# Edge attention on one core: where the picking one-hots are made, how many columns are picked by products, and who empties the product bank

## The reference, cut to what matters

```python
h = jnp.maximum(_layernorm(x, axis=-1), 0.0)
# three times, with nf = h at first:
f_out = (nf @ W_ni)[src] + (nf @ W_nj)[dst] + ef @ W_fij + bias
f_out = leaky_relu(f_out, 0.2).reshape(-1, H, D)
e = einsum('ehd,hd->eh', f_out, attn)
a = exp(e - segment_max(e, dst)[dst]); a = a / segment_sum(a, dst)[dst]
hn = (nf @ W_node).reshape(-1, H, D)
nf = segment_sum(hn[src] * a[:, :, None], dst).mean(axis=1)
ef = f_out.mean(axis=1)
# at the end: x + nf
```

## Time and profile before

| | |
|---|---|
| median of 3 runs | 2908.23 us (2904.49 to 2915.27) |
| profiled execution, its own time | 2908.63 us |
| its span in the profile | 2906.8 us |
| TensorE busy | 2274.3 us, 78% |
| VectorE busy | 2435.2 us, 84% |
| ScalarE busy | 1503.3 us, 52% |
| GpSimd busy | 2060.1 us, 71% |
| mean granted clock of TensorE | 0.892 |

### The profile page before, as it was taken

How to read it: one execution, slowest core, us unless ns; L and a number is a source line. 1 busy time by engine, 2 the same in 40 slices (tenths; PEclk the granted TensorE clock), 3 DMA queues, 4 the chain that set the end, 5 groups by cost and what they waited for, 6 DMA issues and landing times.

```text
span 2906.8 us, 49919 instructions
## 1 busy us (share of the span) xinstructions
PE 2274.3 (78%) x15871; PEld 1753.4 (60%) x16027; DVE 2435.2 (84%) x5972; ACT 1503.3 (52%) x3713; POOL 2060.1 (71%) x2167
## 2 busy tenths in 40 slices
PE   3388888888888468888888887836888888888884
PEld 1266666666665356666666665535767666666653
DVE  7299999999997458999999998736898899898874
ACT  0056565656565225656565655613555555555552
POOL 6777777777772577777777777567777777777753
PEclk9699999999998689899999999958898898898885
DMA  7235454545442324444444443333334343343322
GB/s 256 69 97 160 116 158 119 161 116 159 118 132 93 106 68 143 118 139 140 138 134 140 142 138 103 106 112 96 103 103 124 115 128 106 114 127 102 103 89 80
DMA packets 139273, 353.90 MB, mean 122 GB/s; under 512 B 43895, under 2 KB 96027, under 8 KB 120207
## 3 DMA queue, kind: packets, MB, share of 16 engines
q1 hardware_dynamic: 67216, 296.09, 28.7%
q0 software_dynamic: 68960, 39.71, 9.3%
q10 hardware_dynamic: 2838, 14.91, 1.3%
HBM read 137.79 MB, written 212.77 MB: 121 GB/s over the span
## 4 chain that ended last, share of the span: by engine, by line
DVE 40%; PE 20%; issue 14%; ACT 12%; POOL 9%; DMA 3%; SPq 1%; DVEq 0%; ACTq 0%; POOLq 0%
DVE U L1383 17%; POOL rows L561 7%; DVE rows L1304 6%; PE f_ps L702 6%; DVE lr L1315 5%; PE f_ps L711 5%; DVE U L1368 4%; PE pick_ps L671 4%; ACT up L928 3%; ACT xT L848 3%; ACT f_low L857 3%; PE xT_ps L692 2%; DVE z L1394 2%; DVE rows L1405 2%; PE f_ps L721 2%
## 5 line engine op out<-in xcount | busy, mean ns | idle before, releaser
L561 POOL DMA_INDIRECT rows<-nf_tab,src_sb x1995 | 1890.8, 948 | 638.0 <-issue 588.0
L711 PEld LDWEIGHTS f_ps<-w_out,lr 128*128 128x128 f32 x4836 | 658.8, 201 | 357.7 <-issue 201.2
L1383 DVE TENSOR_TENSOR_SCAN U<-wide_ps,U 128x272 f32<-128x272 f32 (+2 forms) x1272 | 801.3, 692 | 3.3 <-ACT wide_ps L916 2.4
L702 PE MATMUL f_ps<-xT,w_edge 97*128 97x512 f32 x1212 | 697.7, 659 | 39.1 <-ACT ef_new L879 26.3
L671 PE MATMUL pick_ps<-nf_part,z 125*128 125x160 bf16 x6345 | 565.2, 247 | 208.4 <-issue 166.5
L671 PEld LDWEIGHTS pick_ps<-nf_part,z 125*128 125x128 bf16 x6345 | 507.8, 104 | 236.7 <-issue 189.7
L711 PE MATMUL f_ps<-w_out,lr 128*128 128x36 f32 (+1 forms) x4836 | 627.4, 269 | 27.2 <-DVE lr L1315 24.7
L1315 DVE TENSOR_TENSOR lr<-f_ps,f_low 128x512 f32<-128x512 f32 x606 | 407.5, 672 | 203.6 <-ACT f_low L857 202.9
L857 ACT ACTIVATE f_low<-f_ps 128x512 f32<-128x512 f32 x606 | 361.6, 597 | 325.6 <-PE f_ps L702 325.5
L692 PE MATMUL xT_ps<-ident,rows 128*97 128x128 f32 x2418 | 416.1, 297 | 92.1 <-issue 37.0
L916 ACT ACTIVATE wide_ps<-e_dw 128x289 f32<-128x289 f32 (+2 forms) x636 | 245.3, 402 | 348.7 <-DVE U L1383 343.0
(11 more groups left out here) (162 smaller groups left out, 1148.5 us busy)
## 6 DMA issues: line engine op xcount, KB each, us to landing
u_tab<-up SPq DMA_DIRECT2D x144, 1088.0 KB, 4.5
s_nd<-edge_first SPq DMA_DIRECT2D x48, 768.0 KB
rows<-nf_tab,src_sb POOLq DMA_INDIRECT x1995, 2.4
ef_tab<-ef_new SPq DMA_DIRECT2D x32, 768.0 KB
ef_st<-ef_tab SPq DMA_DIRECT2D x32, 768.0 KB
z<-fifth_tab SPq DMA_DIRECT2D x141, 96.0 KB
edge_first<-s_nd ACTq DMA_DIRECT2D x16, 768.0 KB
ef_st<-in_edge_attr_dram SPq DMA_DIRECT2D x16, 672.0 KB
```

Source lines behind the costliest of these rows:

```text
L561: eng.indirect_dma_start(rows[q % RING][:, c * K:c * K + D], None, nf_tab[:, :], bass.IndirectOffsetOnAxis(ap=src_sb[:, t:t + 1], axis=0)) ...
L702: eng.matmul(f_ps[n % 2][:, 0:grp_w(g) * P], w_edge[l][:, :], xT[y][0:K, 0:grp_w(g) * P], start=True, stop=True).then_inc(f_ready, 1)
L711: mm = eng.matmul(f_ps[n % 2][:, u * m:(u + 1) * m], lr[y][:, u * P:(u + 1) * P], w_out[l][:, 0:m], start=True, stop=True)
L1383: last = eng.tensor_tensor_scan(uh[:, c0 * w:c1 * w], dbc[h % 2][:, 0:(c1 - c0) * w], uh[:, c0 * w:c1 * w], 0.0, ALU.mult, ALU.add)
```

## The change

Every group from 6 to 182 has its column 2 picked (a batch is column 2 of three consecutive groups), and the first six groups have all four columns picked (eight batches, one for each column of three groups); a layer so has 67 batches and 605 gathers, not 47 and 665. Batches are picked nine ahead (START). The one-hots are made in the first layer alone: SP stores each to `hot_tab`, and in layers two and three loads it back (`load_hot`); three one-hot tiles take the place of two, two tiles of loaded columns the place of four. `take_picks` gains a second ScalarE copy, of the other four candidates to `pick_sb` in SBUF; `pick_rows` reads from there, and TensorE waits for both copies (`drained`) in place of VectorE's overwrites.

```diff
-LEAD = 8
-LEAD0 = 20
+LEAD = 14
+LEAD0 = 26
-HEADC = 48
-HEADM = 56
-HEAD_PACE = {16: 3, 24: 8, 32: 13, 40: 18}
+HEADC = 72
+HEADM = 80
+HEAD_PACE = {32: 3, 44: 8, 56: 13, 64: 18}
-IDXB = 4
+IDXB = 2
+HOTS = 3
+FRONT = 6
...
-    NPICK = END // GB + 1
+    WHOLE = FRONT // PICK * GT
+    AHEAD = 3
+    NPICK = WHOLE + (END - FRONT) // PICK
+    PEND = FRONT + (END - FRONT) // PICK * PICK
+    START = WHOLE - FRONT // PICK + AHEAD
...
+    hot_tab = nc.dram_tensor("hot_tab", (NPICK * NQ, PARTS5 * PICK * P), BF16, kind="Internal").ap()
...
+        pick_sb = sb("pick_sb", [P, PICK * (PB - D)])
+        rest4 = pick_sb[:, :].rearrange("p (c b d) -> p c b d", b=PARTS5 - 1, d=D)
...
         def is_picked(t):
-            return t % GT == 2 and picks(t // GT)
+            return t < FRONT * GT or (t % GT == 2 and t < PEND * GT)
...
+                def store_hot(b):
+                    eng.wait_ge(hot_made, PARTS5 * (b + 1))
+                    eng.dma_start(hot_tab[b * NQ:(b + 1) * NQ, :], hot[b % HOTS][0:NQ, :]
+                                  ).then_inc(hot_out[b % HOTS], 16)
+                def load_hot(l, b):
+                    m = l * NPICK + b
+                    eng.wait_ge(pick_ready, PICK * (m - HOTS + 1))
+                    if m < NPICK + HOTS:
+                        eng.wait_ge(hot_out[m % HOTS], 16 * -(-(NPICK - m % HOTS) // HOTS))
+                    eng.dma_start(hot[m % HOTS][0:NQ, :], hot_tab[b * NQ:(b + 1) * NQ, :]
+                                  ).then_inc(hot_in[m % HOTS], 16)
+                def bring(l, b):
+                    if l:
+                        load_hot(l, b)
+                        return
+                    m = b
                     if m >= IDXB:
-                        eng.wait_ge(hot_made, PARTS5 * (m - IDXB + 1))
+                        store_hot(m - IDXB)
                     eng.dma_start(fifths[m % IDXB],
...
-                    for b in range(IDXB + 2):
-                        load_fifths(l, b)
+                    loaded = START - 2 if l else IDXB + 2
+                    for b in range(loaded):
+                        bring(l, b)
                     load_first(q0)
                     load_first(q0 + 1)
+                    for b in range(loaded, START + 5):
+                        bring(l, b)
+                    loaded = START + 5
...
                             store_u(k0 + b)
-                            if b + IDXB + 2 < NPICK:
-                                load_fifths(l, b + IDXB + 2)
+                            while loaded < min(START + (GB * b + 9) // PICK + 3, NPICK):
+                                bring(l, loaded)
+                                loaded += 1
...
                     def pick(b, i):
                         m = l * NPICK + b
-                        eng.wait_ge(hot_made, PARTS5 * (m + 1))
                         if i == 0:
-                            eng.wait_ge(picked, PARTS5 * m)
+                            if l == 0:
+                                eng.wait_ge(hot_made, PARTS5 * (m + 1))
+                            else:
+                                eng.wait_ge(hot_in[m % HOTS], 16 * hot_loads(m))
                             eng.wait_ge(parted, 4 * (l + 1))
                             if m == 0:
                                 eng.wait_ge(fifth_copied, 2)
+                            else:
+                                eng.wait_ge(drained, 2 * m)
...
-                        b, i = g // GB + 2, g % GB
-                        if g >= 0 and i < PICK and b < NPICK:
+                        b, i = g // PICK + START, g % PICK
+                        if g >= 0 and b < NPICK:
                             pick(b, i)
...
-                        eng.activation(picked_rows(q, b), pick4[:, :, 0, :], ACT.Copy
-                                       ).then_inc(picked, 1)
+                        eng.activation(picked_rows(l, b), pick4[:, :, 0, :], ACT.Copy
+                                       ).then_inc(drained, 1)
+                        if m:
+                            eng.wait_ge(picked, (PARTS5 - 1) * m)
+                        eng.activation(rest4, pick4[:, :, 1:PARTS5, :], ACT.Copy
+                                       ).then_inc(drained, 1)
...
-                        if g >= 0 and i == PICK - 1 and g // GB + 2 < NPICK:
-                            take_picks(g // GB + 2)
+                        if g >= 0 and g % PICK == PICK - 1 and g // PICK + START < NPICK:
+                            take_picks(g // PICK + START)
                         if g >= 0 and g % GS == 2 and g // GS + 1 < NS:
                             put_ef(g // GS + 1)
...
                     def make_hot(b):
-                        m = l * NPICK + b
+                        m = b
                         eng.wait_ge(fifth_in[m % IDXB], 16 * (m // IDXB + 1))
-                        if m >= 2:
-                            eng.wait_ge(pick_ready, PICK * (m - 1))
+                        if m >= HOTS:
+                            eng.wait_ge(pick_ready, PICK * (m - HOTS + 1))
+                            eng.wait_ge(hot_out[m % HOTS], 16 * (m // HOTS))
...
-                            eng.wait_ge(picked, PARTS5 * m + v)
+                            if v == 1:
+                                eng.wait_ge(drained, 2 * (m + 1))
+                            else:
+                                eng.wait_ge(picked, (PARTS5 - 1) * m + v - 1)
...
-                                pick4[:, :, v, :]).then_inc(picked, 1)
-                    make_hot(0)
-                    make_hot(1)
-                    pick_rows(0)
-                    make_hot(2)
-                    pick_rows(1)
+                                rest4[:, :, v - 1, :]).then_inc(picked, 1)
+                    if l == 0:
+                        make_hot(0)
+                        make_hot(1)
+                    for b in range(START):
+                        if l == 0 and b + 2 <= START:
+                            make_hot(b + 2)
+                        pick_rows(b)
                     slice_b(0)
                     spread_dst(0, range(D))
...
-                        if g >= 0 and i == PICK - 1 and b + 3 < NPICK:
-                            pick_rows(b + 3)
-                        if g >= 0 and i == 0 and b + 4 < NPICK:
-                            make_hot(b + 4)
+                        m = g // PICK + START
+                        if g >= 0 and g % PICK == PICK - 1 and m < NPICK:
+                            pick_rows(m)
+                        if l == 0 and g >= 0 and g % PICK == 0 and m + 1 < NPICK:
+                            make_hot(m + 1)
```

More of the change, by code:

```diff
@@ L186, in egat_kernel @@
         HOTW = PARTS5 * PW // 2
-        hot = [z[:, a * HOTW:(a + 1) * HOTW].bitcast(BF16) for a in range(2)]
-        fifths = [z[:, 2 * HOTW + a * PW // 2:2 * HOTW + (a + 1) * PW // 2].bitcast(FP16)
+        hot = [z[:, a * HOTW:(a + 1) * HOTW].bitcast(BF16) for a in range(HOTS)]
+        fifths = [z[:, HOTS * HOTW + a * PW // 2:HOTS * HOTW + (a + 1) * PW // 2].bitcast(FP16)
                   for a in range(IDXB)]
@@ L247, in egat_kernel @@
         hot_made = sem("hot_made")
+        hot_out = [sem(f"hot_out{a}") for a in range(HOTS)]
+        hot_in = [sem(f"hot_in{a}") for a in range(HOTS)]
+        drained = sem("drained")
         pick_ready = sem("pick_ready")
@@ L340, in ef_in_count, with batch_col, batches_to, hot_loads @@
             return 16 * sum(ef_loads(a) for a in range(q % 2, q + 1, 2))
-        def picks(g):
-            return g % GB < PICK and g // GB < NPICK
         def is_picked(t):
-            return t % GT == 2 and picks(t // GT)
+            return t < FRONT * GT or (t % GT == 2 and t < PEND * GT)
         def gathered(g):
-            return grp_w(g) - picks(g)
+            return sum(not is_picked(t) for t in range(g * GT, g * GT + grp_w(g)))
+        def batch_col(b):
+            if b < WHOLE:
+                return b // GT * PICK * GT + b % GT
+            return FRONT * GT + (b - WHOLE) * PICK * GT + 2
+        def batches_to(g):
+            if g < FRONT:
+                return (g // PICK + 1) * GT
+            return WHOLE + (g - FRONT) // PICK + 1
+        def hot_loads(m):
+            return sum(a % HOTS == m % HOTS for a in range(NPICK, m + 1))
         def rows_sem_to(q, a):
@@ L619, in gather_z @@
                                                    ).then_inc(z_in[a], 16)
+                    if l == 0:
+                        for a in range(HOTS):
+                            eng.wait_ge(hot_out[a], 16 * -(-(NPICK - a) // HOTS))
                     early = ZEARLY if l == L - 1 else len(part_cols[0])
@@ L683, in turn @@
                             eng.wait_ge(ef_put, q + 1)
[L684 to L686 removed]
+                        if rows_sem_to(q, a):
+                            eng.wait_ge(src_rows[q % RING][a], rows_sem_to(q, a))
+                        if g < PEND:
```

(7 more changed lines are left out.)

40 lines of the change are left out of this document (22 added, 18 removed).

## The result

The changed kernel takes 3761.21 us (median of four runs), the kernel before 2906.36 in the same rounds: a ratio of 1.292, 95% interval 1.287 to 1.297. Three of the four runs took 3749.43 to 3763.19 us; the fourth took 7908.36, for a reason that the record does not show, and the ratio leaves it out. The prediction, 3490 us with a range of 3200 to 3640, had the direction, and was 271 us too low.

What follows compares the result with a forecast made beforehand. GpSimd and VectorE nearly tied, layer one at VectorE's pace. Layer one 112 + 156 + 25, layer two 74 + 40, layer three 43 + 40, fronts 92: +582 on 2908.63 gives 3490 us, range 3200 to 3640.

Steps and rivals of the forecast that it cites:

- The drain's wait of 4.5 us: TensorE idles 4.5 us at group 5 of twelve, as ScalarE's lay-out stands ahead of the copies emptying the product bank.
- VectorE's waits of 9 and 3 us: Layer one: VectorE waits 9 us, and one step later 3, for column loads queued behind U and a one-hot store.
- the term's 156: Layer one's loop: thirteen periods with both column waits, 12 us each, add 156 us; bounds 66 and 278.
- Layer one's front: Nine batches picked ahead of the first scan, not two, make layer one's first activation 38 us later.
- The queued 480 KB of 125 rows: A one-hot store or reload on SP's queue takes 4.27 us, at 112 KB/us from the nearest profiled load.
- the 1.1 of the fit: The skill's 2.0 us + bytes/436e3 gives 1.1 us for a queued 480 KB transfer; the prediction preferred the profiled row.
- the one-hots lie in a hole: VectorE's one-hots, 1.26 us, fill its wait for ScalarE behind the scores' softening, so removing them saves much less.
- It adds 1.4 us, right behind the wait. Two idles above 3 us per period now: TensorE's slow clock after idles slows pick and turn: 40 us in layers two and three each, 25 in layer one.
- the 80 named as a bound: Upper bound of the clock term: 80 us a layer if the whole pick, edges and scores run slow.
- rival 3: Layers two and three: one-hot reloads come late in a queue shared with U, five more us per period, 3640; chance 0.10.
- the walk: Starts traced through each engine's program order over twelve groups; gives layers two and three 53.9 us a period.
- The fronts of layers two and three: Nine one-hot reloads queue behind nf_tab's store ahead of the first scan: first activations 27 us later in each layer.

Runs made afterwards that it cites:

- e2: Changed kernel with each batch's one-hot and column transfers issued ahead of the store of U on SP's queue: 3454.43 us, ratio 1.184.
- b1: Kernel before, making only the first two sets of one-hots in layers two and three and picking every batch with them: 2879.54 us, ratio 0.992.
- e4: Changed kernel with twelve unused TensorE products ahead of the waiting pick in three of twelve steps: 3609.12 us, ratio 1.237.
- e5: Changed kernel with bank-emptying copies right behind the lowering, batch transfers ahead of the store of U, and 128 partitions for 125: 3166.85 us, ratio 1.091.
- h1: Kernel before, one-hots stored in layer one and loaded later, 128 partitions, ahead of the store of U, two steps or more early: 2880.62 us, ratio 0.991.
- h3: Kernel before with stored and loaded one-hots, two steps or more early, but 125 partitions and behind the store of U: 2894.34 us, ratio 0.996.
- e3: Changed kernel with one-hot stores and loads of 128 partitions, three rows unused, in place of 125: 3500.65 us, ratio 1.200.
- e7: Changed kernel with bank copies behind the lowering, transfers ahead of the store of U, 128 partitions, no wholly picked first groups: 3088.86 us, ratio 1.064.

## Why the prediction was wrong

**Right.** The drain's wait of 4.5 us (4.38). VectorE's waits of 9 and 3 us: 10.34 and 2.47, 13.0 a period in layer one for a forecast 12, and thirteen waits of 9.8 to 11.3 us in all; e2, which takes them away, gains 182 us there for the term's 156. Layer one's front (34.4 for 38). The queued 480 KB of 125 rows: 4.27 us taken, some 4.1 by the queue's rate at layer two's start, far from the 1.1 of the fit. (In the Trainium skill that fit stands in DMA: Bandwidth & Descriptors, Anatomy of one DMA, and is for transfers on GpSimd's path; these are SyncE's.) The chain of waits of the changed kernel has the landings, 9.74, 10.18 and, for the long wait, 8.98 us for 9.6:

```profile
310.02 9.74 DMA z<-fifth_tab
...
328.67 10.18 DMA z<-fifth_tab
...
357.09 8.98 DMA z<-fifth_tab
```

That the saving is small was right as well (b1). That it is small because the one-hots lie in a hole is shown only in part: GpSimd's gathers, without a gap in both kernels, alone hold the mean period of layer two near 48.7 us. In a period shorter than that the gathers must have been ahead, and the shortest periods that recur there went from about 48.2 to 47.4 us, some 0.8 for the 3.78 that VectorE was spared.

**The step that failed: "It adds 1.4 us, right behind the wait. Two idles above 3 us per period now".** The drain's two idles are there (4.38 and 3.38 us in the period shown), and the reload adds a third (3.27). But behind each the low level holds longer than over the pick and the turn that the prediction charged, from a pick and most of its edges up to a whole round (pick, edges, scores, turn) and the next pick and edges: 1.6 to 4.6 us of TensorE's time each. e4, with most of the low level gone, has a period of 57.8 us where the changed kernel mostly has 64.8: 7.0 us, net of the added products, against 2.6 taken. Its loops of layers two and three are 78.3 and 75.4 us shorter, where the sum had 40 each; that is near the 80 named as a bound. The row from which the 1.4 us came was a mild case. In the same trace, 9 us earlier, a wait of 1.45 us is followed by a slow pick and slow edges:

```profile
1100.42 1.88 PE L671 MATMUL pick_ps<-nf_part,z 125*128 125x160 bf16 x15
1102.09 2.00 PE L702 MATMUL f_ps<-xT,w_edge 97*128 97x512 f32 x2
```

**The term that was left out: rival 3.** The reloads do come late in layers two and three. TensorE waits 171.2 us for them in all: 53.9 in layer two's loop (3.2 to 6.1 us a period in its steady part) and 80.2 in layer three's (5.3 a period), where the rival had five. The prediction weighed the queue's load, 286 us of a layer; what counts is when a batch is issued and when it is needed. SyncE's queue and TensorE in the changed kernel:

```profile
1908.79 0.32 SPq L476 DMA_DIRECT2D u_tab<-up  x1
1909.16 0.86 SPq L457 DMA_DIRECT2D z<-hot_tab  x2
```

```profile
1918.01 2.18 PE L727 MATMUL pick_ps<-nf_part,z 125*128 125x160 bf16 x15 [3.27 <-DMA z<-hot_tab]
```

Two loads go out behind the store of U, and TensorE is free 5.6 us later (1918.01 - 3.27 - 1909.16). This is the third idle. For layer two's usual period, 53.9 us of the walk, 7.0 of the clock and 3.3 of the reload make 64.2 for the 64.8 measured. By layers, layer two is 79 us over its forecast, against 38 of the clock (78.3 less the 40 taken) and 53.9 of the reloads; layer three is 113 over, against 35 and 80.2. The two overlap (an earlier reload also spares a slow round), so this shows the size, not an exact split.

**Layer one** is 70 us over. Without column waits (e2) its period is 61.4, where the walk had 55.4 before any clock; with the drain moved up and 128 rows as well it is 54.5 (e5). So about 6 us a period belong to the drain and the clock behind it, where the sum had 1.6 for the clock; in the changed kernel itself e4 gained only 15 us there. How they divide was not settled.

**The fronts of layers two and three** (+40.7 and +33.1 for 27 each): the batches go at 4.09 us apiece through product and drain, and the last two are queued behind edge_first. With two batches ahead and 128 rows (h1) the starts are as before.

The walk of the programs' order, then, gave the wait and its length; what it lacked was the length of the slow clock behind each wait and a term for each transfer that must land within two steps.

## What to carry to other kernels

Where a single buffer is refilled in every step, look at what the emptying instruction stands behind in its engine's program: here moving two copies by one step was worth 70 us, ahead of any change to their cost. A saving on a full engine is worth what the next engine leaves of it: GpSimd's gathers left no gap beside VectorE's 95%, and leaving out 90 sets of one-hots bought 0.8%. Bring what is needed two steps ahead and it may be slow (h3's ratio is 0.996 where h1's is 0.991); bring it in the step in which it is needed and its length is paid (128 rows in place of 125 gave 260 us in e3).

## What the runs showed of the hardware that was not expected

Behind waits of equal length (4.38 and 4.37 us) two picks, what lies between them and most of the next edges ran at the low level in one case, one pick and most of its edges in the other. Waits of 1.90 and 2.56 us (in e7, the picks at 1715.27 and 1742.06) are already followed by a slow round:

```profile
1715.27 2.16 PE L725 MATMUL pick_ps<-nf_part,z 125*128 125x160 bf16 x15 [1.90 <-ACT pick_sb L966]
1717.22 1.99 PE L757 MATMUL f_ps<-xT,w_edge 97*128 97x512 f32 x2
...
1742.06 2.16 PE L725 MATMUL pick_ps<-nf_part,z 125*128 125x160 bf16 x15 [2.56 <-ACT pick_sb L966]
```

125 rows in place of 128 cost the core's DMA traffic more than half of its speed while the reloads ran (some 135 GB/s for some 350). And VectorE's overwrite was no shorter from SBUF than from PSUM: 278 ns on average in the changed kernel, 268 in the kernel before.
